# A fused attention and expert-layer kernel: four operand tiles moved by 32 bytes against the 64-byte lines of the weights

## The chip, the cores and the metric

The program runs on one NeuronCore of a Trainium2 chip. Its metric is the device time of one execution in microseconds. One execution was taken by the hardware profiler; its rows are quoted below. PE is TensorE (matmuls), PEld its weight loads, DVE is VectorE, ACT is ScalarE, POOL is GpSimd, SP is the engine that issues most DMAs.

## The reference

Input x is 2 x 2048 x 1024 in float32.

1. A convolution over the sequence with 3 taps, 1024 channels in and 768 out; its output is cut into q, k and v of 256 channels each.
2. Block attention: blocks of 128 tokens, 16 heads of 64. `qh = q @ wq + bq`, the same for k and v; scores scaled by 1/8, causal mask, softmax, `o = p @ v`; the heads' outputs times `wo` plus `bo` (256 wide), then `@ proj_w + proj_b` (1024 wide).
3. `x = layernorm(x + attention)`.
4. `base = x @ W_base.T + b_base`; a gate softmax over 8 experts minus a threshold, clipped and normed; `h = x @ A` (8 experts of rank 16), weighted by the gate, times `B`, times 2.
5. `out = layernorm(x + base + moe)`.

## The kernel before

**Products in two parts.** Every float32 operand of a large product is split into HI (`activation(Copy)` to float32r by ACT) and LO (raw minus HI, by DVE or POOL), and the product is made in three passes, `PASSES = ((HI, HI), (HI, LO), (LO, HI))`. A `matmul(out, stationary, moving)` is two instructions in the trace: a weight load (PEld) of the stationary operand, 128 x 128, and a MATMUL that streams the moving operand, 256, 266, 384 or 512 columns. Both read SBUF. The load for the next matmul runs while the matmul before it streams.

**Stages.** (a) Convolution, about 14 to 455 us: three sweeps over 4 units of 1024 tokens, 4 steps of 2 channel chunks each (48 steps of 72 matmuls, line 598), with 256 columns, stationary from `weights`, moving from `x_split`. (b) Attention, about 455 to 1035 us: `tile(t)` for 8 tiles of 512 tokens, each with 8 head pairs `s`. Per pair PE does: project_qk of the pair after next (line 1119: 6 matmuls into bankh for k and 6 into banka for q; stationary the weights, moving the split convolution tile `cs`), make_scores (line 1133), weigh_v (line 1158), transpose_probs (line 1145), project_v (line 1104: stationary `cs`, moving the weights), add_out (line 1168: stationary `wo`, moving the heads' outputs `oT`). (c) The last stage, about 1035 to 1620 us: 32 blocks of 128 tokens. Per block PE does: base (line 1525: stationary the transposed block `x1T`, moving the weights `wf`, in column ranges of 512, 384 and 266, each over 8 chunks and 3 passes), transpose_x1 (line 1515), transpose_h (line 1534), project (line 714: stationary `ys`, the tile `y_split`, moving `wp`), experts (line 1542: stationary `hT`, the tile `h_weighted_T`, moving `wb`).

**Order.** Each engine runs a program of its own, written out by hand; semaphores join them. No planner decides anything.

**Where things lie.** All large weights lie in one tile, `weights` (`attn.arena`), first the convolution's, later those of attention, `cs`, and those of the last stage, each at an offset written in the code. The tile begins at byte 16512 of a partition (a multiple of 64, and of 128). Behind it come the staging tiles and small ones, and then `scratch`, at byte 145728 (a multiple of 64, and 64 past a multiple of 128), in which `attn.at(name, ..., offset)` places everything else by hand. So before the change, modulo 64 bytes: the convolution weights 0, `x_split` 0, the attention weights 0, `cs` 0, `oT` 0, `x1T` 0, `hT` 0, `wb` 0, `wp` 0, `y_split` 32, `identity` 32, the first x1 tile (`v_bias_rows`) 32, the second (`x_odd`) 0. A row of `wf` is 1162 elements (4648 bytes), so its chunks begin at 0, 16, 32, 48, 0, 16 (HI, chunks 0 to 5) and 40, 56, 8, 24, 40, 56 (LO); chunks 6 and 7 lie in `late_weights` at 0 and 16 (HI), 40 and 56 (LO).

Of the kernel before, what the change touches and what calls it, by code (L numbers as in the profile page):

```python
# [8 lines left out]
F32 = mybir.dt.float32  # L9
F32R = mybir.dt.float32r  # L10
# [4 lines left out]
P = 128  # L15
BATCH, SEQ, DM = 2, 2048, 1024
# [8 lines left out]
ST = 512  # L25
# [4 lines left out]
CC = DM // P  # L30
CF = 3 * WB // P
KC = WB // P
HP = HEADS // 2
XS = 3
WCOLS = DM + ER + EXPERTS + 2
# [9 lines left out]
FP = CF // 2  # L45
CHUNK = 2 * 2 * CF * P
ARENA = CC * CHUNK
MASK_ROWS = P // QUAD
MASK_STORES = QUAD
SCRATCH = 20880  # L50
SMALL = 79968
SCORE_SMALL = 80128
Phase = namedtuple("Phase", "sync gpsimd scalar vector tensor")
# [13 lines left out]
class AttentionStart:  # L67
# [7 lines left out]
    NW = KC * HE  # L75

    def __init__(self, ctx, nc):
        def sb(name, shape, dt):
            return ctx.enter_context(nc.sbuf_tensor(name, shape, dt))

        def sem(name):
            return ctx.enter_context(nc.semaphore(name))

        NW, TILE = self.NW, CF * ST
        self.banks = [ctx.enter_context(nc.psum_tensor(f"bank{chr(97 + i)}", [P, ST], F32)) for i in range(8)]
        self.arena = sb("weights", [P, ARENA], F32R)
        self.stages = sb("weight_stage", [P, 2 * WCOLS], F32)
        self.stage = self.stages[:, 0:NW]
        self.craw = sb("conv_tile", [P, CF, ST], F32)
        self.out = sb("features_out", [P, KC, ST], F32)  # L90
        self.mask = sb("causal_mask", [P, P], F32)
        self.ident = sb("identity", [P, P], F32)
        self.bq, self.bk = sb("q_bias", [P, HP], F32), sb("k_bias", [P, HP], F32)
        self.bv, self.bo = sb("v_bias_rows", [P, HE], F32), sb("o_bias", [P, KC], F32)

        self.start = [2 * NW * n for n in range(3)] + [6 * NW + 2 * TILE]
        self.w = [self.arena[:, a:a + 2 * NW].rearrange("p (i n) -> p i n", i=2) for a in self.start]
        self.cs = self.arena[:, 6 * NW:6 * NW + 2 * TILE].rearrange("p (i f n) -> p i f n", i=2, f=CF)

        self.bias_loaded = sem("attn_bias_loaded")  # L100
        self.wv_loaded, self.stage_loaded = sem("wv_loaded"), sem("weight_stage_loaded")
        self.w_hi, self.w_lo = sem("attn_w_hi"), sem("attn_w_lo")
        self.zeroed, self.masks = sem("attn_zeroed"), sem("attn_masks")
        self.c_loaded = sem("conv_tile_loaded")
        self.c_hi, self.c_lo = sem("conv_tile_hi"), sem("conv_tile_lo")
        self.stored = sem("stored")
        self.y_stored = [sem(f"conv_y_stored{i}") for i in range(2)]
        self.evac, self.fin_done = sem("conv_evacuated"), sem("conv_finished")

        self.base = (nc.sbuf_base + 31) // 32 * 32  # L110
        sb("scratch", [P, SCRATCH], F32)
        self.nc = nc

    def at(self, name, shape, dt, offset):

        assert 0 <= offset and offset + 4 * math.prod(shape[1:]) <= 4 * SCRATCH, name
        return self.nc.alloc_sbuf_tensor_at(name, shape, dt, offset=self.base + offset)


def conv_phase(ctx, nc, xT, conv_w, conv_b, convT, attn, attn_w, q_bias, k_bias, v_bias, o_bias):  # L120
# [30 lines left out]
    def sem(name):  # L151
        return ctx.enter_context(nc.semaphore(name))

    w = attn.arena[:].rearrange("p (c i k n) -> p c i k n", c=CC, i=2, k=2)
    craw = attn.craw[:].rearrange("p f n -> p (f n)")
    wraw = [craw[:, 0:TAPS * KTAPS].rearrange("p (k n) -> p k n", k=TAPS),
            attn.stages[:, 0:TAPS * KTAPS].rearrange("p (k n) -> p k n", k=TAPS)]
# [7 lines left out]
    mbuf = attn.at("conv_m", [P, 2, 2 * 2 * UQ], F32, 36864)  # L165
    mask4 = attn.at("mask_by_phase", [MASK_ROWS, QUAD, P], F32, 77888)
    bias = attn.at("conv_bias", [P, CF], F32, 79936)
# [41 lines left out]
    def sync(sp):  # L209
# [75 lines left out]
        def store_masks():  # L285
            sp.wait_ge(attn.masks, MASK_STORES + 1)
            for r in range(MASK_STORES):
                sp.dma_start(attn.mask[r * MASK_ROWS:(r + 1) * MASK_ROWS, :], mask4[:, r, :]).then_inc(stored, 16)

# [58 lines left out]
    def gpsimd(pool):  # L348
# [4 lines left out]
        for r in range(QUAD):  # L353
            rows = mask4[:, r, :].rearrange("p (k n) -> p k n", k=QUAD)
            nc.gpsimd.affine_select(out=rows, in_=rows, compare_op=ALU.is_ge, fill=MASKED, base=r,
                                    pattern=[[-1, QUAD], [-QUAD, MASK_ROWS]],
                                    channel_multiplier=QUAD).then_inc(attn.masks, 1)
# [80 lines left out]
    def vector(dve):  # L438
# [85 lines left out]
        def finish_second(u, p):  # L524
# [7 lines left out]
            else:  # L532
                dve.wait_ge(y_stored[e % 2], 32 * (e // 2))
            a = m[(FP * u + p) % 2].rearrange("p f k (b j) -> p f k b j", j=MASK_ROWS)
            l = L[e % 2].rearrange("p i f k (b j) -> p i f k b j", j=MASK_ROWS)
            y = Y[e % 2].rearrange("p f (b k j) -> p f b k j", k=QUAD, j=MASK_ROWS)
            y = [y[:, :, :, k, :] for k in range(QUAD)]
# [100 lines left out]
class FfnStart:  # L638
# [8 lines left out]
    def __init__(self, ctx, nc, attn, proj_w, ffn_w, lora_b):  # L647
        def sem(name):
            return ctx.enter_context(nc.semaphore(name))

        def parts(a, n):
            return attn.arena[:, a:a + 2 * n].rearrange("p (i n) -> p i n", i=2)


        qk = attn.at("q_and_k", [P, 2, 2, ST], F32, 0)
        self.k, self.q = qk[:, 0, :, :], qk[:, 1, :, :]
        late = attn.at("late_weights", [P, self.LATE * 2 * WCOLS], F32R, 45056)
        second, kept = attn.start[1], CC - self.LATE
        self.wp = [parts(attn.start[attn.WV] + 2 * DM * k, DM) for k in range(KC)]
        self.wf = [parts(second + 2 * WCOLS * k, WCOLS) for k in range(kept)]  # L660
        self.wf += [late[:, 2 * WCOLS * k:2 * WCOLS * (k + 1)].rearrange("p (i n) -> p i n", i=2) for k in range(self.LATE)]
        self.wb = parts(attn.start[attn.WO] + 2 * attn.NW, DM)

        wo = attn.start[attn.WO]
        self.x1T = attn.arena[:, wo:wo + 4 * DM].rearrange("p (i h k n) -> p i h k n", i=2, h=2, k=CC)
        self.stage = [attn.stages[:, i * WCOLS:(i + 1) * WCOLS] for i in range(2)]
        self.stage.append(attn.at("weight_stage2", [P, WCOLS], F32, 63648)[:])

        f = [(ffn_w[k], self.wf[k], WCOLS) for k in range(CC)]
        p = [(proj_w[k], self.wp[k], DM) for k in range(KC)]  # L670
        self.weights = [(lora_b, self.wb, DM)] + p + f
        self.AFTER_V, self.AFTER_QK = 1, 1 + KC
        self.KEPT = len(self.weights) - self.LATE

        raw = attn.craw[:].rearrange("p f n -> p (f n)")
        self.xt = raw[:, 0:2 * DM].rearrange("p (i n) -> p i n", i=2)
        self.yr = raw[:, 2 * DM:2 * DM + 2 * KC * P].rearrange("p (i k n) -> p i k n", i=2, k=KC)
        self.ys = attn.at("y_split", [P, 2, 2, KC, P], F32R, 68320)
        self.pb = attn.at("proj_b_rows", [P, DM], F32, 72416)

        self.w_loaded = [sem(f"ffn_w_loaded{i}") for i in range(STAGES)]
        self.w_hi = sem("ffn_w_hi")
        self.w_lo = [sem(f"ffn_w_lo{n}") for n in range(len(self.weights))]
        self.pb_loaded = sem("proj_b_loaded")
        self.x_loaded = [sem(f"x_tile_loaded{i}") for i in range(2)]
        self.y_loaded = [sem(f"y_loaded{i}") for i in range(2)]
        self.xb_ready = sem("x_plus_bias_ready")
        self.y_hi, self.y_lo = sem("y_hi"), sem("y_lo")
        self.attn_stored = attn.stored
        self.proj_done = sem("proj_done")  # L690
        self.res1_ready = sem("res1_ready")


        small = attn.at("ln_small", [P, 34], F32, SMALL)
        self.stats = small[:, 0:24].rearrange("p (k h n) -> p k h n", k=2, h=2)
        self.mv = small[:, 24:28].rearrange("p (k n) -> p k n", k=2)
        self.var_eps, self.rstd = small[:, 28:30], small[:, 30:32]
        self.minus_half, self.eps = small[:, 32:33], small[:, 33:34]
        self.consts = sem("ln_consts_ready")
        self.ln_step = [sem(f"ln{k + 1}_step") for k in range(2)]  # L700
        self.var_ready = [sem(f"ln{k + 1}_var_ready") for k in range(2)]
        self.rstd_ready = [sem(f"ln{k + 1}_rstd_ready") for k in range(2)]
        self.stats_seen = sem("ln_stats_seen")
        self.x1_ready = sem("x1_ready")
        self.first_x1 = attn.bv
# [45 lines left out]
def attention_phase(ctx, nc, convT, attn, yT, ffn, x, y_blocks, proj_b):  # L751
# [11 lines left out]
    w, cs, craw = attn.w, attn.cs, attn.craw  # L763
# [4 lines left out]
    q, k = ffn.q, ffn.k  # L768
# [2 lines left out]
    ntop = attn.at("score_neg_max", [P, 2, 2 * BLK], F32, SCORE_SMALL + 64)  # L771
    total = attn.at("prob_sum", [P, 2, 2 * BLK], F32, SCORE_SMALL + 128)
    inv = attn.at("prob_inv_sum", [P, 2, 2 * BLK], F32, SCORE_SMALL + 192)
    oT = attn.at("heads_out", [P, 2, 2, ST], F32R, 36864)
    probsT = attn.at("probs_T", [P, 2, ST], F32, 32768)
    y = attn.out[:, 0:KC, :]
    ps_qt, ps_kt = attn.banks[0], attn.banks[7]
# [452 lines left out]
def ffn_phase(nc, x, yT, attn, ffn, b_base, b_thr, out):  # L1230

    with ExitStack() as ctx:
# [20 lines left out]
        wts = attn.at("gate_weights", [P, EXPERTS], F32, 33536)  # L1253
        wsum = attn.at("gate_sum", [P, 3], F32, 33568)
        hw = attn.at("h_weighted", [P, ER], F32, 33600)
        hT = attn.at("h_weighted_T", [P, 2, P], F32R, 34112)
        ps_a = attn.banks[0:2]
        ps_f = [attn.banks[2:5], attn.banks[5:8]]
        HT0 = LAST
# [409 lines left out]
```

## Time and profile before

| | |
|---|---|
| median of 3 runs | 1622.99 us (1621.26 to 1624.43) |
| the profiled execution | 1622.18 us, its span 1620.1 us |
| PE busy | 1555.3 us, 96% of the span, 10816 matmuls |
| PEld busy | 1387.3 us, 86% |
| DVE busy | 1183.7 us, 73% |
| ACT busy | 610.4 us, 38% |
| POOL busy | 263.4 us, 16% |

The span runs from the first to the last instruction; the device time is 2.1 us longer. A matmul's recorded duration holds a part that overlaps the next matmul, so what one costs in a dense stretch is the spacing from start to start, which the views of the timeline give.

### The profile page before, as it was taken

What the parts mean: (1) busy time and instruction counts of PE and PEld (TensorE: products, weight loads), DVE (VectorE), ACT (ScalarE), POOL (GpSimd) and SP (SyncE); (2) the same over time, 40 slices, a digit from 0 to 9 for tenths busy, and PEclk for the clock granted to TensorE, in tenths of its full rate; (3) what the DMA queues carried; (4) which work ended last, traced back from release to release, by engine and by line L of the source; (5) the groups of instructions that cost most, each with busy time, mean ns of one, the idle gap of its engine ahead of it and who ended that gap; (6) DMA issues with size and microseconds to landing.
All of it is one profiled execution on the core that took longest, in us unless ns stands there. A gap on an engine that the chain in (4) does not pass through costs nothing. (4 is left out here: it accounts for less than half of the span.)

```text
span 1620.1 us, 29293 instructions
## 1 busy us (share of the span) xinstructions
PE 1555.3 (96%) x10816; PEld 1387.3 (86%) x10816; DVE 1183.7 (73%) x2785; ACT 610.4 (38%) x1729; POOL 263.4 (16%) x230
## 2 busy tenths in 40 slices
PE   6998999699979999999999999899999999999997
PEld 6998999699968878888888888789898989998997
DVE  6858867687686666666666667777888788878884
ACT  4223322322257676676777677511111111111110
POOL 0000000000011010100101011533333333333331
PEclk9999999799999999999999999899999999999999
DMA  7887664677850001010110112412111211121111
GB/s 293 327 291 267 215 220 167 213 259 266 287 197 7 24 31 52 0 52 0 52 52 0 52 58 83 134 59 75 59 58 63 82 59 58 58 84 62 58 43 52
DMA packets 55157, 181.05 MB, mean 112 GB/s; under 512 B 5552, under 2 KB 13872, under 8 KB 48432
## 3 DMA queue, kind: packets, MB, share of 16 engines
q1 hardware_dynamic: 53360, 173.81, 30.6%
q10 hardware_dynamic: 1728, 6.29, 1.0%
q8 instruction: 47, 0.77, 0.2%
q14 instruction: 22, 0.18, 0.0%
HBM read 125.49 MB, written 54.53 MB: 111 GB/s over the span
## 5 line engine op out<-in xcount | busy, mean ns | idle before, releaser
L919 ACT ACTIVATE scores_and_probs<-scores_and_probs,score_neg_max 128x128 f32<-128x128 f32 x512 | 198.1, 393 | 1.6 <-DVE score_neg_max L1017 1.6
L1012 DVE CUSTOM_DVE_ANT_0 scores_and_probs<-bankb,causal_mask 128x128 f32<-128x128 f32 x256 | 59.2, 287 | 119.1 <-PE bankc L1133 116.7
L1361 ACT ACTIVATE gate_exp<-h_and_gate,gate_neg_max 128x8 f32<-128x8 f32 x32 | 9.6, 301 | 348.9 <-DVE gate_neg_max L1436 348.9
L366 ACT ACTIVATE x_split<-x_planes 128x1024 fp32r<-128x1024 f32 x48 | 51.0, 1062 | 202.4 <-PE bankf L598 152.7
L1104 PE MATMUL bankg<-weights 128*128 128x512 f32 x384 | 106.1, 412 | 1.8 <-DVE v_heads L1002 1.5
L886 POOL TENSOR_TENSOR weights<-conv_tile,weights 128x1024 fp32r<-128x1024 f32 x14 | 35.8, 2556 | 435.4 <-ACT weights L905 350.4
L486 DVE TENSOR_TENSOR x_split<-x_planes,x_split 128x1024 fp32r<-128x1024 f32 x48 | 58.7, 1222 | 64.2 <-ACT x_split L366 63.9
L1119 PE MATMUL bankh<-weights 128*128 128x512 f32 x384 | 99.0, 393 | 1.4 <-DVE weights L561 1.4
L1119 PE MATMUL banka<-weights 128*128 128x512 f32 x384 | 98.3, 391 | 0.7
L598 PE MATMUL banka<-x_split,weights 128*128 128x256 f32 x576 | 79.0, 285 | 20.3 <-DVE weights L508 14.2
L919 ACT ACTIVATION_READ_ACCUMULATOR scores_and_probs<-scores_and_probs,score_neg_max 128x1 f32 x512 | 98.3, 192 | 0.0
L598 PE MATMUL banke<-x_split,weights 128*128 128x256 f32 x576 | 77.6, 282 | 21.1 <-ACT conv_m L399 12.8
L598 PEld LDWEIGHTS banka<-x_split,weights 128*128 128x128 f32 x576 | 72.7, 193 | 22.2 <-issue 22.1
L598 PEld LDWEIGHTS banke<-x_split,weights 128*128 128x128 f32 x576 | 72.2, 192 | 21.6 <-ACT conv_m L399 13.0
L1119 PEld LDWEIGHTS bankh<-weights 128*128 128x128 f32 x384 | 72.0, 188 | 18.9 <-DVE weights L561 1.8
L1119 PEld LDWEIGHTS banka<-weights 128*128 128x128 f32 x384 | 71.5, 188 | 18.6 <-POOL weights L886 3.3
L731 DVE BATCH_NORM_STATS2 ln_small<-residual_sum 128x6 f32<-128x512 f32 x126 | 81.1, 685 | 5.9 <-DVE residual_sum L725 4.6
L879 POOL TENSOR_TENSOR weights<-weight_stage,weights 128x512 fp32r<-128x512 f32 x4 | 6.9, 1750 | 464.7 <-ACT weights L983 464.7
L1024 DVE TENSOR_TENSOR scores_and_probs<-scores_and_probs,prob_inv_sum 128x1024 f32<-128x1024 f32 x64 | 80.4, 1256 | 2.2
L1133 PEld LDWEIGHTS bankb<-q_and_k 64*128 64x128 f32 x512 | 61.7, 187 | 22.6 <-issue 22.6
L1104 PEld LDWEIGHTS bankg<-weights 128*128 128x128 f32 x384 | 68.3, 191 | 14.2 <-DVE v_heads L1002 2.0
L598 PE MATMUL bankb<-x_split,weights 128*128 128x256 f32 x576 | 77.5, 282 | 0.0
(229 smaller groups left out, 3975.0 us busy)
## 6 DMA issues: line engine op xcount, KB each, us to landing
x_raw<-in_xT SPq DMA_DIRECT2D x32, 1028.0 KB, 7.2
conv_tile<-in_x SPq DMA_DIRECT2D x32, 512.0 KB, 3.7
out<-out_tile SPq DMA_DIRECT2D x32, 512.0 KB, 2.7
conv_tile<-convT_scratch SPq DMA_DIRECT2D x16, 768.0 KB, 6.5
conv_tile<-in_conv_w SPq DMA_DIRECT2D x8, 1152.0 KB, 7.4
weight_stage<-in_conv_w SPq DMA_DIRECT2D x8, 1152.0 KB, 9.3
ce_scratch<-conv_l SPq DMA_DIRECT2D x16, 512.0 KB, 8.4
x_planes<-ce_scratch SPq DMA_DIRECT2D x16, 512.0 KB, 4.5
```

What stands on the lines that cost most here:

```text
L366: nc.scalar.activation(xs[:, j % XS, HI], T[:, j % 2, 0:2], ACT.Copy).then_inc(x_hi, 1)
L486: nc.vector.tensor_tensor(xs[:, j % XS, LO], T[:, j % 2, 0:2], xs[:, j % XS, HI].bitcast(F32), ALU.subtract).then_inc(x_lo, 1)
L598: last = nc.tensor.matmul(acc[f][:, k, :], w[:, c, a, k, f * P:(f + 1) * P], xs[:, j % XS, b, k, c % CPG, :], start=(c == 0 and k == 0 and ...
L731: nc.vector.bn_stats(self.stats[:, k, h, :], src[:, h * ST:(h + 1) * ST]).then_inc(step, 1)
L886: nc.gpsimd.tensor_tensor(cs[:, LO, a:b, :], craw[:, a:b, :], cs[:, HI, a:b, :].bitcast(F32), ALU.subtract).then_inc(c_lo, 1)
L919: last = nc.scalar.activation(probs[:, s % 2, i, :], probs[:, s % 2, i, :], ACT.Exp, bias=ntop[:, s % 2, i:i + 1], scale=SCORE_SCALE, accu ...
L1012: last = nc.vector.tensor_tensor_reduce(out=probs[:, s % 2, i, :], in0=ps_s[h][:, n * P:(n + 1) * P], in1=mask[:], scale=1.0, scalar=LOWES ...
L1024: nc.vector.tensor_tensor(probs[:, s % 2, :, :], probs[:, s % 2, :, :], inv[:, s % 2, :].unsqueeze(2).broadcast_to([P, 2 * BLK, P]), ALU.m ...
L1104: last = nc.tensor.matmul(ps_v[:], cs[:, a, V[0] + kc, b * P:(b + 1) * P], wqkv(attn.WV, c, kc, cols), start=(i == 0), stop=(i == 5))
L1119: last = nc.tensor.matmul(out[:], wqkv(weight, a, kc, slice(s * P, (s + 1) * P)), cs[:, c, part[0] + kc, :], start=(i == 0), stop=(i == 5))
L1133: last = nc.tensor.matmul(ps_s[j][:, cols], q[rows(j), s % 2, cols], k[rows(j), s % 2, cols], start=True, stop=True)
L1361: nc.scalar.activation(ge[:], hg[:, ER:ER + EXPERTS], ACT.Exp, bias=ngm[:, 0:1], accum_out=den[:, 0:1]).then_inc(ge_ready, 1)
```

## The change

The tile `weights` grows by 32 elements (128 bytes), and with it everything behind it moves by 128 bytes. `scratch` gets 30 elements shorter. `ODD` is 8 elements (32 bytes), `LINE` 16 elements (64 bytes).

- `cs` begins `ODD` later: modulo 64 bytes it is at 32, the attention weights at 0.
- `oT` (`heads_out`) goes from offset 36864 to 36896: at 32.
- `x1T` begins `LINE + ODD` later: at 32. `hT` goes from 34112 to 34144: at 32.
- `wo`, `wb` and the convolution weights move by one or two `LINE`s; `late_weights`, `weight_stage2`, `y_split` and `proj_b_rows` move by 64 bytes inside `scratch`. Modulo 64 these stay where they were; modulo 128 the convolution weights go from 0 to 64 while `x_split` stays at 64.

No instruction is added, taken away or put in another order, and no loop, wait, size or queue differs.

```diff
+ODD, LINE = 8, 16
-SCRATCH = 20880
+SCRATCH = 20850
-        self.arena = sb("weights", [P, ARENA], F32R)
+        self.arena = sb("weights", [P, ARENA + 2 * LINE], F32R)
-        self.start = [2 * NW * n for n in range(3)] + [6 * NW + 2 * TILE]
+        self.start = [2 * NW * n for n in range(3)] + [6 * NW + 2 * TILE + LINE]
-        self.cs = self.arena[:, 6 * NW:6 * NW + 2 * TILE].rearrange("p (i f n) -> p i f n", i=2, f=CF)
+        self.cs = self.arena[:, 6 * NW + ODD:6 * NW + ODD + 2 * TILE].rearrange("p (i f n) -> p i f n", i=2, f=CF)
-    w = attn.arena[:].rearrange("p (c i k n) -> p c i k n", c=CC, i=2, k=2)
+    w = attn.arena[:, LINE:LINE + ARENA].rearrange("p (c i k n) -> p c i k n", c=CC, i=2, k=2)
-        late = attn.at("late_weights", [P, self.LATE * 2 * WCOLS], F32R, 45056)
+        late = attn.at("late_weights", [P, self.LATE * 2 * WCOLS], F32R, 45120)
-        self.wb = parts(attn.start[attn.WO] + 2 * attn.NW, DM)
+        self.wb = parts(attn.start[attn.WO] + 2 * attn.NW + LINE, DM)
-        self.x1T = attn.arena[:, wo:wo + 4 * DM].rearrange("p (i h k n) -> p i h k n", i=2, h=2, k=CC)
+        self.x1T = attn.arena[:, wo + ODD:wo + ODD + 4 * DM].rearrange("p (i h k n) -> p i h k n", i=2, h=2, k=CC)
-        self.stage.append(attn.at("weight_stage2", [P, WCOLS], F32, 63648)[:])
+        self.stage.append(attn.at("weight_stage2", [P, WCOLS], F32, 63712)[:])
-        self.ys = attn.at("y_split", [P, 2, 2, KC, P], F32R, 68320)
-        self.pb = attn.at("proj_b_rows", [P, DM], F32, 72416)
+        self.ys = attn.at("y_split", [P, 2, 2, KC, P], F32R, 68384)
+        self.pb = attn.at("proj_b_rows", [P, DM], F32, 72480)
-    oT = attn.at("heads_out", [P, 2, 2, ST], F32R, 36864)
+    oT = attn.at("heads_out", [P, 2, 2, ST], F32R, 36896)
-        hT = attn.at("h_weighted_T", [P, 2, P], F32R, 34112)
+        hT = attn.at("h_weighted_T", [P, 2, P], F32R, 34144)
```

## Rows read from the trace of the kernel before

**Rows 1.** The page, parts 1 and 2: PE's busy time and its 40 slices.
```profile
PE 1555.3 (96%) x10816; PEld 1387.3 (86%) x10816; DVE 1183.7 (73%) x2785; ACT 610.4 (38%) x1729; POOL 263.4 (16%) x230
...
PE   6998999699979999999999999899999999999997
...
PEclk9999999799999999999999999899999999999999
```
**Rows 2.** Busy time by stretch: length, engines, granted clock, DMA share, GB/s.
```profile
26.00:94.00 68.00, 66.83 (x569) 66.38 (x568) 53.12 (x72) 21.58 (x25) 0.00 (x0) 1.00 0.89 341
...
500.00:980.00 480.00, 479.25 (x3522) 388.57 (x3521) 315.66 (x1273) 335.49 (x1137) 40.65 (x16) 1.00 0.09 32
1060.00:1580.00 520.00, 520.00 (x2937) 468.52 (x2936) 420.69 (x779) 66.34 (x202) 180.06 (x173) 1.00 0.18 63
```
**Rows 3.** The page, part 4: the chain that ended last, by engine.
```profile
PE 36%; DVE 0%; POOLq 0%; issue 0%; POOL 0%; DVEq 0%
```
**Rows 4.** Timeline of PE in attention: start us, length us, line, tiles, count.
```profile
882.13 0.86 PE L1168 MATMUL banke<-heads_out,weights 128*128 128x512 f32 x3
882.83 0.86 PE L1168 MATMUL bankf<-heads_out,weights 128*128 128x512 f32 x3
883.53 1.54 PE L1119 MATMUL bankh<-weights 128*128 128x512 f32 x6
884.91 1.52 PE L1119 MATMUL banka<-weights 128*128 128x512 f32 x6
```
**Rows 5.** Matmuls of 512 columns by line: count, duration in ns min/median/max, first and last start.
```profile
L1119 PE MATMUL bankh<-weights x384: 387/393/534, 456.6 to 1005.1; 128*128 128x512 f32 x192
L1119 PE MATMUL banka<-weights x384: 387/389/504, 458.1 to 1006.5; 128*128 128x512 f32 x192
...
L1168 PE MATMUL bankf<-heads_out,weights x192: 390/394/398, 498.8 to 1030.3; 128*128 128x512 f32 x192
...
L1104 PE MATMUL bankg<-weights x384: 387/395/775, 453.6 to 995.1; 128*128 128x512 f32 x192
...
L714 PE MATMUL bankb<-weights,y_split x180: 392/394/399, 1055.5 to 1580.4; 128*128 128x512 f32 x180
```
**Rows 6.** The same view of the last stage, lines 1525 and 1542.
```profile
L1525 PE MATMUL bankc<-weights x288: 388/394/403, 1043.4 to 1589.2; 128*128 128x512 f32 x144
L1525 PE MATMUL bankd<-weights x288: 332/337/423, 1049.8 to 1594.7; 128*128 128x384 f32 x144
L1525 PE MATMUL banke<-weights x288: 280/285/340, 1040.5 to 1584.3; 128*128 128x266 f32 x144
...
L1525 PE MATMUL bankc<-late_weights,weights x96: 387/392/402, 1047.6 to 1590.5; 128*128 128x512 f32 x96
L1525 PE MATMUL bankd<-late_weights,weights x96: 331/334/338, 1053.1 to 1595.8; 128*128 128x384 f32 x96
L1525 PE MATMUL banke<-late_weights,weights x96: 280/290/292, 1042.7 to 1585.1; 128*128 128x266 f32 x96
...
L1542 PE MATMUL bankc<-weights,h_weighted_T x48: 389/395/398, 1056.9 to 1596.4; 128*128 128x512 f32 x48
```
**Rows 7.** Groups in 1206.1 to 1210.8 us: chunks 0, 2 and 6 of `wf`; busy, mean ns.
```profile
L1525 PE MATMUL bankf<-weights 128*128 128x512 f32 x3 | 0.9, 397 | 0.0
...
L1525 PE MATMUL bankf<-weights 128*128 128x512 f32 x3 | 0.9, 394 | 0.0
...
L1525 PE MATMUL bankf<-late_weights,weights 128*128 128x512 f32 x3 | 0.8, 391 | 0.0
```
**Rows 8.** Line 598 in two stretches of the convolution: min/median/max ns.
```profile
L598 PE MATMUL bankb<-x_split,weights x36: 276/281/281, 69.9 to 88.6; 128*128 128x256 f32 x36
...
L598 PE MATMUL bankb<-x_split,weights x36: 276/276/281, 103.7 to 121.9; 128*128 128x256 f32 x36
```
**Rows 9.** Transposes of the last stage against `identity`: min/median/max ns.
```profile
L1515 PE MATMUL banka<-identity,v_bias_rows x60: 272/272/273, 1067.0 to 1573.0; 128*128 128x128 f32 x60
...
L1515 PE MATMUL banka<-identity,x_odd x56: 272/273/273, 1085.1 to 1555.0; 128*128 128x128 f32 x56
```

## The prediction

> **What bounds the kernel now.** I read the page first: PE is busy 96% of the span and its slices are at 9 nearly throughout, at the full granted clock [rows 1]. The table of stretches says where it counts: in attention PE is busy 479.25 of 480 us, in the last stage 520.00 of 520, against 315.66 and 420.69 for DVE and 335.49 and 66.34 for ACT [rows 2]; the chain that ended last is PE for its whole 36% of the span, which is the last stage [rows 3]. The convolution is nearly as dense, 66.83 of 68 us, with DMA at a share of 0.89 beside it [rows 2]. So a nanosecond per matmul is a nanosecond per matmul of the end, in attention and behind it; the convolution passes it on only while DMA keeps up.
>
> The change touches no instruction, only addresses. The question is therefore what a matmul costs and whether that depends on where its operands lie. The timeline gives the spacing: line 1168 does 3 matmuls in 0.70 us (882.13 to 882.83), 233 ns each; line 1119's k part does 6 in 1.38 us, 230 ns [rows 4]. Their recorded durations are 394 and 393 ns [rows 5], so a duration is the spacing plus about 162 ns, and differences of durations are differences of cost. I use durations from here.
>
> Matmuls of one shape do not cost the same: with 512 columns they go from 387 to 399 ns, with medians of 389 (q projection), 393 (k), 394 (line 1168, and line 714 with y_split) and 395 (lines 1104 and 1542) [rows 5, 6]. In the convolution the same instruction runs at 276 in one stretch and at 281 in another, with the same operands relative to a line [rows 8]. So something lets a matmul run at two levels or between, and neither the shape nor the address alone picks it. Each matmul streams while the next one's weights are loaded; that these two reads get into each other's way is the plain reading, and it is what moving one of them could change.
>
> **What the rows say of 32 bytes.** There are places where the offset of 32 stands already. Line 714 has y_split at 32 against wp at 0: median 394, lowest 392, no better than line 1168 at offset 0 and worse than the q projection, also at 0 [rows 5]. In line 1525 chunk 2 of wf begins at 32 (HI) and 8 (LO): mean 394; chunk 0 at 0 and 40: 397; but chunk 6, at 0 and 40 as well: 391 [rows 7]. The same phase stands 3 ns above and 3 ns below the offset of 32. The transposes take 272 and 273 ns with identity and source both at 32, and with one at 32 and one at 0 [rows 9]. So the trace shows no law "32 apart is cheap"; it shows levels into which a sequence of matmuls settles.
>
> The Trainium skill speaks against the change altogether: its page "SBUF — State Buffer", section "Who interferes with whom", gives PE two independent SBUF read ports, one for the moving operand and one for weight loads, and says PE never waits on anyone. By that rule no address matters, and the sum would be 0. The rows agree for the transposes [rows 9] and not for the two levels of line 598 [rows 8], which need some cause.
>
> **The change part by part.** The trace has no row of the new placement, so each term is bounded by the lowest and highest durations of its own shape; I take the middle between the two levels that rows show as medians, 389 and 394, that is 391.5, because moving an operand draws the level anew and nothing favours one.
>
> - k and q projection (moving cs at 32): 384 x (393 - 391.5) = 0.6 us gained and 384 x (391.5 - 389) = 1.0 lost: +0.4. Bounds: all at 387, -3.1; all at 398, +5.4.
> - v projection (stationary cs): the first matmul of each six starts after another wait, so 320 count: 320 x (391.5 - 395) = -1.1. Bounds -2.6 and +1.0.
> - add_out, line 1168 (moving oT): 384 x (391.5 - 394) = -1.0. Bounds -2.7 and +1.5.
> - Line 1525, 512 columns (stationary x1T): 576 from weights x (391.5 - 394) = -1.4; 192 from late_weights x (391.5 - 392) = -0.1. Bounds -5.0 and +3.5.
> - 266 columns: ends 280 and 292, middle 286: 576 x (286 - 285) = +0.6, 192 x (286 - 290) = -0.8. Bounds -4.8 and +4.4.
> - 384 columns: medians 337 (338 in bankg) and 334, lowest 331, highest 346 in line 1542 with this shape; no second level is visible, so I take 0. Bounds -4.3 and +7.2.
> - Line 1542 (stationary hT): 96 x (391.5 - 395) = -0.3; bounds with its 384-column part -1.4 and +1.1.
> - Convolution: weights and x_split keep their phase in 64 bytes, though their distance in 128 bytes changes from 64 to 0. I take 0. If placement decides its level after all, each of its 12 units of 288 matmuls can flip by 5 ns, 1.4 us; the medians are 281, so at least half is at the upper level: from -17 to +8.6. Kept as a tail.
> - The writers of the moved tiles (ACT for HI, DVE and POOL for LO): no row shows the new placement. In attention DVE is idle 164 us of 480 and ACT 145, in the last stage DVE 99 of 520 [rows 2], which hides a third more time on ACT and DVE in attention and a fifth on DVE behind it; without that cover each per cent on DVE's 315.66 us would be 3 us. Taken as 0. No DMA touches cs, oT, x1T or hT; weight_stage2 and proj_b_rows are loaded once.
>
> Sum: 0.4 - 1.1 - 1.0 - 1.5 - 0.2 - 0.3 = -3.7 us. From the profiled execution's own 1622.2 us that is 1618.5; the median shown is 0.8 above that execution, so 1619.3, and I say **1619**. Bounds without the convolution: about -24 and +24, 1599 and 1647.
>
> **The rivals.** A: *the offset really keeps the reads apart*, and every changed product falls to the lowest duration of its shape. That is the -24 in full; 387 and 280 are reached today by single matmuls, so a real effect would bring most of them there, say 14 us: 1609 (between 1599 and 1615). For it: spacing varies by up to 12 ns within one line with nothing else changed. Against it: y_split and chunk 2 [rows 5, 7]. B, on the other side: *the q and k projections lose the level they have settled in*. They are the cheapest today, and moving cs puts them and their neighbours at the top of their shape: 384 x 9 + 384 x 5 = 5.4 us for line 1119, 1.5 for line 1168, 1.0 for line 1104, 7.9 together: 1631. It decides as soon as the q projection's median rises from 389 to about 396. For it: line 714, with an offset of 32, never goes under 392. Against it: it must hit three lines at once. C: *the change doesn't do what it says*, since addresses play no part (the page's rule above): 1623, and every median stays.
>
> **How the numbers follow.** Forecast 0.38, A 0.30, B 0.20, C 0.12. The forecast's own range is 1614 to 1625. The range of 8 in 10 goes from 1604 to 1631: it leaves out the lower end of A, a strong B, and a convolution that flips as a whole. Under 0.2% (3.2 us) a difference is none that a measurement of this kernel tells from no change. Faster by more: all of A and half of the forecast, 0.30 + 0.20 = 0.50. Within: 0.15 of the forecast and C, 0.27. Slower: B and the rest, 0.23.
>
> **What would show it right or wrong.** Counts stay at 10816 matmuls. By the forecast line 1119's banka rises from 389 towards 391 or 394, line 1168 falls below 394, and line 1525 has medians within 3 ns of today's. By A the medians of 1119, 1168, 1104 and 1525 go to 387 to 389 together, and line 714, whose offset is unchanged, stays at 394. By B 1119 goes to 396 or more. By C nothing moves by over 1 ns. I am wrong altogether if line 598 changes level in most units, or if PE is no longer busy 479 of 480 us in attention.

## The result: 13 us slower, and the time is in the convolution

| | median of the runs | against before |
|---|---|---|
| before | 1622.51 us (1619.04 to 1624.43, 6 runs) | |
| after | 1635.68 us (1633.74 to 1639.65, 6 runs) | ratio 1.0084, 95% interval 1.0068 to 1.0100 |

The profiled execution of the kernel after took 1639.65 us, the longest of its six and 4.0 us above their median; its span is 1637.7 us. The instruction counts are the same. The page of the kernel after answers to [rows 1] with this; the last two lines are PE's slices and its granted clock:

```profile
PE 1570.5 (96%) x10816; PEld 1398.7 (85%) x10816; DVE 1183.9 (72%) x2785; ACT 610.5 (37%) x1729; POOL 262.6 (16%) x230
...
PE   6999899699989999999999999899999999999998
...
PEclk9999999899999999999999999999999999999999
```

PE is busy 15 us longer for the same 10816 matmuls, and its granted clock reads nearly alike in both. Where, the view by line tells (count, min/median/max duration in ns, first and last start). First the convolution after, to [rows 8]:

```profile
L599 PE MATMUL banka<-x_split,weights x576: 278/283/550, 14.0 to 461.7; 128*128 128x256 f32 x192
L599 PE MATMUL bankb<-x_split,weights x576: 277/283/415, 15.4 to 463.1; 128*128 128x256 f32 x192
```

The median went from 281 to 283, which looks small. But the lowest went from 276 to 277 or 278, and the fast stretches are gone. The last start of banka in the convolution was 446.0 us before and is 461.7 now: 15.7 of the 17.6 us of span are lost before attention begins. The timeline of one step of the kernel after gives the spacing (start, length, line, tiles, count):

```profile
99.83 1.48 PE L599 MATMUL bankb<-x_split,weights 128*128 128x256 f32 x11
101.15 1.60 PE L599 MATMUL bankc<-x_split,weights 128*128 128x256 f32 x12
102.59 0.88 PE L599 MATMUL bankd<-x_split,weights 128*128 128x256 f32 x6
```

Bankc's 12 matmuls take 102.59 - 101.15 = 1.44 us, 120.0 ns each. The kernel before shows two spacings, 1.41 us and 1.36 us for 12 matmuls, 117.5 and 113.3 ns each:

```profile
76.96 1.58 PE L598 MATMUL banka<-x_split,weights 128*128 128x256 f32 x12
78.37 0.87 PE L598 MATMUL bankb<-x_split,weights 128*128 128x256 f32 x6
...
94.15 1.52 PE L598 MATMUL banka<-x_split,weights 128*128 128x256 f32 x12
95.51 0.84 PE L598 MATMUL bankb<-x_split,weights 128*128 128x256 f32 x6
```

Taken from the starts of all matmuls of the trace, with the gaps over 130 ns left out (waits), every one of the 48 steps is at 120.0 ns (119.6 at the least); before, 26 steps were at 117.8, 21 near 113.3 and one between. Mean 119.9 against 115.8. Here and below, the first step of a unit can lie some ns off its level.

Then attention and the last stage after, to [rows 5, 6]:

```profile
L1120 PE MATMUL bankh<-weights x384: 389/396/497, 472.3 to 1023.6; 128*128 128x512 f32 x192
L1120 PE MATMUL banka<-weights x384: 388/396/500, 473.8 to 1025.0; 128*128 128x512 f32 x192
...
L1169 PE MATMUL bankf<-heads_out,weights x192: 388/397/420, 514.5 to 1048.8; 128*128 128x512 f32 x192
...
L1105 PE MATMUL bankg<-weights x384: 389/394/774, 469.5 to 1013.4; 128*128 128x512 f32 x192
...
L715 PE MATMUL bankb<-weights,y_split x180: 394/396/400, 1072.7 to 1597.9; 128*128 128x512 f32 x180
...
L1526 PE MATMUL bankc<-weights x288: 387/394/407, 1060.6 to 1606.6; 128*128 128x512 f32 x144
L1526 PE MATMUL bankd<-weights x288: 331/337/426, 1066.9 to 1612.2; 128*128 128x384 f32 x144
L1526 PE MATMUL banke<-weights x288: 282/286/338, 1057.6 to 1601.8; 128*128 128x266 f32 x144
...
L1526 PE MATMUL bankc<-late_weights,weights x96: 392/396/398, 1064.8 to 1608.0; 128*128 128x512 f32 x96
```

The q projection's median rose from 389 to 396, k's from 393 to 396. Line 1526 has the medians of before within 1 ns where it reads `weights`; against `late_weights` with 512 columns it rose from 392 to 396, and with 266 it fell from 290 to 286. Summed over starts: q +2.3 us, k +0.9, line 1526 +0.8 with 512 columns (all of it against `late_weights`) and -0.5 with 384 and 266, the other lines together -1.4. PE is as full as before in both stages:

```profile
500.00:980.00 480.00, 479.29 (x3512) 386.37 (x3510) 313.69 (x1272) 332.67 (x1126) 40.47 (x16) 1.00 0.10 34
1080.00:1600.00 520.00, 520.00 (x2932) 467.65 (x2932) 420.07 (x782) 66.36 (x202) 177.14 (x171) 1.00 0.19 63
```

So nearly all of the loss is in a stage that the change was not aimed at. In the tables below the **distance** is the start of the moving operand minus the start of the stationary one, exactly, in bytes modulo 256. For x_split and the convolution weights it was 158016 - 16512 = 141504, which is 192; after the change it is 158144 - 16576 = 141568, which is 0. (All steps inside the two tiles are multiples of 512.)

### The profile page after: what moved, and what is told of

The parts are those of the page before. It is cut to its first block and busy times, and to the rows that moved or that the text cites. A ratio compares the mean times of both kernels' runs of the same rounds, so it can differ in the third digit from the quotient of the medians.

```text
span 1637.7 us, 29293 instructions
## 1 busy us (share of the span) xinstructions
PE 1570.5 (96%) x10816; PEld 1398.7 (85%) x10816; DVE 1183.9 (72%) x2785; ACT 610.5 (37%) x1729; POOL 262.6 (16%) x230
## 5 line engine op out<-in xcount | busy, mean ns | idle before, releaser
L1013 DVE CUSTOM_DVE_ANT_0 scores_and_probs<-bankb,causal_mask 128x128 f32<-128x128 f32 x256 | 59.2, 287 | 121.8 <-PE bankc L1134 119.3
L1120 PEld LDWEIGHTS bankh<-weights 128*128 128x128 f32 x384 | 71.7, 188 | 19.6 <-DVE weights L562 1.6
L599 PE MATMUL bankb<-x_split,weights 128*128 128x256 f32 x576 | 80.8, 288 | 0.0
```

What stands on the lines that cost most here:

```text
L599: last = nc.tensor.matmul(acc[f][:, k, :], w[:, c, a, k, f * P:(f + 1) * P], xs[:, j % XS, b, k, c % CPG, :], start=(c == 0 and k == 0 and ...
L1013: last = nc.vector.tensor_tensor_reduce(out=probs[:, s % 2, i, :], in0=ps_s[h][:, n * P:(n + 1) * P], in1=mask[:], scale=1.0, scalar=LOWES ...
L1120: last = nc.tensor.matmul(out[:], wqkv(weight, a, kc, slice(s * P, (s + 1) * P)), cs[:, c, part[0] + kc, :], start=(i == 0), stop=(i == 5))
```

## The experiments

The theory, D: a matmul's spacing follows from the distance between what it streams and the weights loaded beside it, in more than a 64-byte line. The rivals: the 32-byte moves cost the time (E), any shift of scratch does (F), or the levels are chance of timing (T).

**1. The convolution's distance undone in the kernel after**, but not exactly: it becomes 64, where the kernel before has 192.

```diff
-    xs = attn.at("x_split", [P, XS, 2, 2, CPG, UQ], F32R, 12288)
+    xs = attn.at("x_split", [P, XS, 2, 2, CPG, UQ], F32R, 12352)
```

with the convolution's other tiles behind it, and the small ones, 128 bytes later.

> The kernel after, with one thing undone: x_split starts 64 bytes later in the scratch tile (the tiles of the convolution behind it 128 bytes later, to make room), so that it is again 64 bytes away from the convolution weights modulo 128. Theory D (the distance of the moving operand from the next weights, taken modulo 128 bytes, sets the spacing of a matmul): the convolution's spacing goes from 120.0 back to a mix of 113.3 and 117.8 ns, its 3456 matmuls take about 439 us in place of 455, the whole 1620 to 1624 us. Rival E (the 32-byte moves of cs, heads_out, x1T and hT are what costs, and the convolution merely varies from program to program): the convolution stays where it is or varies by itself, the whole stays at 1636 us. Rival F (any shift of scratch by 128 bytes costs): stays at 120.0 ns and 1636 us.

Measured 1629.03 us (9 runs), ratio 1.0035 (1.0014 to 1.0056): about half of the way back, and 5 us above the 1620 to 1624 expected. The 120.0 is gone from all steps: 35 steps at 117.8, 12 at 113.3 and one between in the profiled execution. Its runs spread from 1620.85 to 1633.03. E and F fail on the convolution; D holds with a mix that is not that of before.

**2. The same distance as after, made in the kernel before.** x_split at 12352 there, nothing of attention or of the last stage touched.

> The kernel before, with x_split alone put 64 bytes further (the convolution's tiles behind it 128 bytes further), so that its distance from the convolution weights is 0 modulo 128 as in the kernel after; cs, heads_out, x1T, hT untouched. Theory D: all 48 steps of the convolution at 120.0 ns, +16 us, 1638 to 1640 us, and the q projection stays at 227 ns. Rival E: 1622 us and a mix of 113.3 and 117.8. Rival F: 1622 us.

All 48 steps at 120.0 ns; the last steps of the timeline read as in the kernel after:

```profile
99.79 1.60 PE L598 MATMUL bankd<-x_split,weights 128*128 128x256 f32 x12
101.23 1.60 PE L598 MATMUL banke<-x_split,weights 128*128 128x256 f32 x12
102.67 0.76 PE L598 MATMUL bankf<-x_split,weights 128*128 128x256 f32 x5
```

The time is 1630.74 us (6 runs), ratio 1.0041 (1.0023 to 1.0059), less than the 1638 to 1640 expected: 3456 x 4.1 ns is 14 us of spacing, its convolution's sum of starts rose by 10.9 (439.5 to 450.4) and the execution by 9.7. The waits in the convolution got shorter by the rest, from 39.2 to 35.9 us. In the medians it is +7.4 us (1623.31 beside it). The profiled execution of the kernel after has the same 120.0 ns and still a sum of 455.5, since its waits are 41.0 us; it is that kernel's slowest run, and what lengthened them is not shown. The convolution's other tiles moved too, by 128 bytes; experiment 9 moves them by the same and x_split by 16 bytes less, and the 120.0 is gone. So it is the move of x_split that makes the slow convolution.

**3 and 4. Two more distances, and cs.** The kernel after with x_split at 32, cs back at 0; and with x_split at 96, cs at 64.

```diff
-        self.cs = self.arena[:, 6 * NW + ODD:6 * NW + ODD + 2 * TILE]
+        self.cs = self.arena[:, 6 * NW + 0:6 * NW + 0 + 2 * TILE]
```

(16 in place of 0 in the second.)

> The kernel after with two moves in two stages, each read in its own: x_split 32 bytes later (32 from the convolution weights modulo 128), and cs at 0 from the attention weights again. Theory D: the q projection is back at 227 ns from 233.6 (line of 384 matmuls, about -2.3 us) and k at 230 from 232.7; the convolution takes a level of its own, which an account by 64-byte lines (odd is good) puts at 113.3 or less and an account by 128 only anywhere from 113.3 to 120. Rival E': the q projection's level comes from what runs around it (oT, wo moved by 64 bytes), then it stays at 233 ns.

> The kernel after with x_split 96 bytes later (96 from the convolution weights modulo 128) and cs at 64 from the attention weights. Theory D: if only the distance modulo 64 counts, this convolution equals that at 32, and the q projection equals cs at 0, 227 ns; if modulo 128 counts, they may differ, and the q projection goes to a level like line 1168's before, 233 ns, whose moving operand was 64 from its weights. Rival: all levels are chance of timing, then convolution steps show a mix of levels whatever the distance.

1633.67 and 1633.25 us (one run each). The convolution is at 116.7 and 117.8 in whole units at distance 32. At 96 single matmuls take 116 to 125 ns in turn, and every step has a mean of 119.8 to 120.1, the level of distance 0:

```profile
100.61 1.60 PE L599 MATMUL bankd<-x_split,weights 128*128 128x256 f32 x12
102.05 1.36 PE L599 MATMUL banke<-x_split,weights 128*128 128x256 f32 x10
```

32 and 96 are not equal, so 64 bytes are not the period. q is at 228.9 ns with cs at 0 and 229.5 with cs at 64, against 233.6 at 32: the move of cs by 32 is what slowed it. But 228.9 is not the 227.2 of before; perhaps what runs ahead of it (line 1169, with oT and wo moved) has a say, which no run shows.

**5 to 8. Other distances in all lines at once.** Each line is read by itself. In these four the rows of wf are also padded, so that all chunks begin at one phase modulo 128. (Not modulo 256: a padded row is 4736 bytes, 18.5 times 256, so HI and LO rows lie 128 apart.)

```diff
+WPITCH = (WCOLS + 31) // 32 * 32
-        self.wf = [parts(second + 2 * WCOLS * k, WCOLS) for k in range(kept)]
+        self.wf = [parts(second + 2 * WPITCH * k, WPITCH)[:, :, 0:WCOLS] for k in range(kept)]
```

> The layout of the kernel after, with other distances (moving minus stationary, modulo 128 bytes), each stage read by itself: convolution 80, k and q projection 16, v projection 112, add_out 16, and in line 1526's place the weight rows padded to 4736 bytes so that all chunks of wf have one phase, distance 0. Theory D (the distance sets the level or the few levels of a line): each line shows one or two spacings; base with 512 columns settles at 227 ns in place of 225 to 236, as the q projection does at distance 0, its sum falls by about 768 x 4.5 = 3.5 us. Rival T (levels are chance of timing, the distance plays no part): base stays at a mean of 231.7 ns and the convolution mixes 113.3 and 117.8.

> As the one before, with distances: convolution 48, k and q projection 48, v projection 80, add_out 48, base 64 with padded rows, experts 64. Theory D: base with 512 columns goes to 233 ns, as add_out at 64 in the kernel before; the convolution lies between 113.3 and 120 with one level per unit. Rival T: as above, no difference between this and the one before.

> As before, with distances: convolution 112, k and q projection 56, v projection 72, add_out 0, base 32 with padded rows, experts 96. Theory D: add_out at 0 goes from 233 to 227 ns, 384 x 6 = -2.3 us; base with 512 columns at the q projection's level for 32, 233 ns. Rival T: add_out stays at 233.

> As before, with distances: convolution 16, k and q projection 8, v projection 120, add_out 64, base 16 with padded rows, experts 80. Theory D: add_out back at 233.4 as in the kernel before; the convolution at 16 near its 120 at distance 0, or between that and 117 at 32. Rival T: a mix of 113.3 and 117.8 in the convolution.

| | time | convolution: distance, mean ns, steps | q at, mean | add_out at, mean | base 512 at (modulo 128), mean |
|---|---|---|---|---|---|
| u_a | 1631.35 | 80: 119.3, 118.3 or 120.0 by unit | 16: 231.3 | 16: 231.2 | 0: 230.0 |
| u_b | 1634.50 | 48: 118.3, all steps | 48: 231.7 | 48: 231.6 | 64: 231.4 |
| u_c | 1616.37 | 112: 113.4, all steps | 56: 232.8 | 0: 230.7 | 32: 231.5 |
| u_d | 1620.21 | 16: 116.6, 113.3 or 118.7 by unit, one unit 116.7 | 8: 233.5 | 64: 231.6 | 16: 232.0 |

(One run each; before took 1618.60 beside them. u_b's convolution has a mean 1.0 ns under u_a's and still a sum of starts 0.7 us above it; the rest is waits.) Rival T falls: the convolution shows its own levels at each distance. Part of what D was to give is refuted as well: add_out at 0 came to 230.7, not to the 227 that the q projection has there, so the distance alone does not fix the level of a short run between other work. For base the test was none. Its mean is 230.0 to 232.0, as with unpadded rows (231.2), but no kernel had it at one distance modulo 256. In u_a its HI times HI matmuls take 231.1 ns from `weights` and 235.0 from `late_weights`, placed alike modulo 128 and 128 apart modulo 256. What the distance rules plainly is the long uniform run of the convolution. And u_c shows a distance at which all 48 steps take 113.3.

**9 to 12. That distance in the kernel before, and the rest of the change alone.** Four kernels, of which three were run 12 times each: the kernel before with x_split 48 bytes further, the kernel after with x_split 112 further, the same with cs back at 0, and, run once, the kernel before with x_split 176 further.

```diff
-    xs = attn.at("x_split", [P, XS, 2, 2, CPG, UQ], F32R, 12288)
+    XN = XS * 2 * 2 * CPG * UQ
+    xs = attn.at("x_split", [P, XN + 32], F32R, 12288)[:, 12:12 + XN].rearrange(
+        "p (s i k c n) -> p s i k c n", s=XS, i=2, k=2, c=CPG)
```

(12 elements here; 28 in the kernel after, 44 in the last.)

> The kernel before with x_split alone 48 bytes later, 112 from the convolution weights modulo 128; everything of attention and the last stage as before. Theory D: all 48 steps of the convolution at 113.3 ns, whatever runs around them, in place of the mix of 113.3 and 117.8: 3456 x (115.8 - 113.4) = 8.3 us of spacing, of which some goes into waits, so 1614 to 1617 us against 1622.5, and a smaller spread from run to run, since the mix is what varies. Rival G (113.3 in the kernel that had 112 came from its other moves): the mix comes back, 1620 to 1624 us.

> The kernel after with x_split at 112 from its weights. The convolution is then the same as in the kernel before with 112, and the difference of the two is what the moves of cs, heads_out, x1T, hT and wo are worth by themselves. Theory D: +2.3 (q) +0.7 (k) +0.8 (line 1526 with 512 columns) -0.8 (266 and 384 columns) and about -1 (other lines): +1.5 to +3 us, 1616 to 1619. Rival E (the 32-byte moves were most of the slowdown): +6 us or more against the kernel before with 112.

> As the one before, with cs back at 0 from the attention weights. Theory D: q from 233.6 to about 229, k from 232.7 to 231, together 1.9 + 0.6 us, so 2 to 3 us faster than the one before and within 1 us of the kernel before with 112. Rival: the two projections are hidden behind other engines, then no difference.

> The kernel before with x_split 128 bytes further than in the one with 112, so 240 from the weights modulo 256 and still 112 modulo 128. Theory D with a period of 128 bytes: all 48 steps at 113.3 ns again. Rival: the period is longer, then another level or mix.

I had counted modulo 128, where the kernel before stands at 64. Exactly it stands at 192, so 48 more is 240 and 176 more is 112, and the texts of the first and the fourth have the two exchanged. The results bear on the period:

| | distance | steps | median, ratio and interval |
|---|---|---|---|
| before, x_split +48 | 240 | 117.1, all | 1624.89; 1.0020 (1.0008 to 1.0032) |
| after, x_split +112 | 112 | 113.3, all | 1618.72; 0.9978 (0.9966 to 0.9989) |
| the same, cs at 0 | 112 | 113.3, all | 1617.16; 0.9967 (0.9958 to 0.9977) |
| before, x_split +176 | 112 | 113.3, all | 1616.04, one run |

112 and 240 are the same modulo 128 and differ, 113.3 against 117.1 ns: 128 is refuted as a period. At 240 the timeline has 1.41 us for 12 matmuls, where at 112 it has 1.36 (shown at the end of this section):

```profile
100.58 1.57 PE L600 MATMUL banke<-x_split,weights 128*128 128x256 f32 x12
101.99 1.45 PE L600 MATMUL bankf<-x_split,weights 128*128 128x256 f32 x11
```

The expectation for the first of the four (1614 to 1617) was missed by 8 us for that reason. The q projection, by the view of groups (busy us, mean ns of one), first of the kernel after with x_split +112:

```profile
L1122 PE MATMUL banka<-weights 128*128 128x512 f32 x384 | 100.6, 397 | 0.7
```

and with cs at 0 as well:

```profile
L1122 PE MATMUL banka<-weights 128*128 128x512 f32 x384 | 98.9, 392 | 0.7
```

The move of cs is shown in the spacing (233.6 to 228.9 for q, 232.7 to 231.3 for k, 2.3 us together). The medians differ by 1.6 us in the direction of that. Their intervals against before overlap, but of the 12 runs with cs at 0 ten lie under 1617.9, and of the 12 with cs at 32 eleven lie above it, so the whole time shows the move too.

**13 to 15. What was still open.**

> The same kernel as the one that was looked at once with x_split 176 bytes further, timed in rounds. Counted exactly, x_split minus the convolution weights is 368 bytes modulo 512 here and in the three kernels after with x_split at 112; in the kernel before with x_split 48 bytes further it was 240, which is 112 modulo 128 as well and gave 117.1 ns. Theory D' (the distance counts modulo more than 128 bytes, 256 or 512): 113.3 ns in all 48 steps again, and since the rest is as before, 1.6 to 4 us faster than the kernel after with 112, 1614 to 1617 us. Rival: the rest of the change was worth nothing, 1618 to 1619 us.

> The kernel before with x_split 320 bytes further: 0 from the convolution weights modulo 512, where the kernel after has 256. If the period is 256 bytes, all 48 steps are at 120.0 ns again; if it is 512 or more, another level shows, perhaps the q projection's good one (17/16 ns per column rate, 113.3).

> The kernel after with the convolution's distance put back exactly to that of the kernel before, 192 modulo 512 (the first attempt at this had 320). Theory D': the mix of 113.3 and 117.8 ns as in the kernel before; the rest costs the +1.5 to 3 us of the moves of cs, heads_out, x1T and hT, so 1623 to 1627 us. Rival (the convolution's slowdown had another source beside the distance): 1629 us or more, as with 320.

*The period.* x_split at 0 modulo 512 (the kernel after has 256 modulo 512): all steps at 120.0 again, 1632.29 us in one run. (The 17/16 in that expectation is no price of a column: 113.3 ns for 256 columns is 0.44 ns each.)

```profile
99.79 1.60 PE L600 MATMUL bankd<-x_split,weights 128*128 128x256 f32 x12
101.23 1.60 PE L600 MATMUL banke<-x_split,weights 128*128 128x256 f32 x12
102.67 0.76 PE L600 MATMUL bankf<-x_split,weights 128*128 128x256 f32 x5
```

0 and 256 agree, 112 and 240 don't: for this line the distance counts modulo 256 as far as these four tell; that a distance and the same plus 256 agree rests on this one pair.

*Distance or address.* One more rival is that x_split's own address sets the level. It lies at 128 modulo 256 in experiments 2, 14 and 15, with 120.0 ns in the first two and the mix in the third, where the weights lie 64 bytes further. And the weights lie at 128 modulo 256 in the kernel before and in experiments 2, 9, 12, 13 and 14, with the mix, 120.0, 117.1 and 113.3 ns among them. Neither address does it alone; the distance fits all.

*The old distance exactly.* The kernel after with x_split 448 bytes further has 192 again. The old mix is back, unit for unit but for the first: its steps 0 to 2 are at 113.3 to 113.5 where 117.8 stood, and units 1, 3, 4, 6, 9 and 11 are at 117.8 (the first step of unit 4 at 116.1) as before. The median of 10 runs is 1625.03, ratio 1.0020 (1.0008 to 1.0031). That is 3.3 us above the runs of before beside it (1621.77). So of the 13.2 us some 10 come back with this one address, and 3.3 stay with everything else that the change moved. The largest part of that rest is q and k with cs at 32, together 3.2 us by their starts in the kernel after:

```profile
L1122 PE MATMUL banka<-weights 128*128 128x512 f32 x384 | 100.6, 397 | 0.7
L1122 PE MATMUL bankh<-weights 128*128 128x512 f32 x384 | 100.4, 397 | 1.3 <-DVE weights L564 1.3
```

*The version that beats both.* The kernel before with x_split alone moved by 176 bytes: 1616.09 us (6 runs, 1614.29 to 1619.56), ratio 0.9965 (0.9951 to 0.9978), 5.7 us under the runs of before beside it (1621.77) and 19.6 under the median of after. Its line 600, and its timeline at the same place, 1.36 us for 12 matmuls, 113.3 ns each:

```profile
L600 PE MATMUL bankb<-x_split,weights x576: 275/275/415, 15.6 to 441.9; 128*128 128x256 f32 x192
```

```profile
100.15 1.52 PE L600 MATMUL bankf<-x_split,weights 128*128 128x256 f32 x12
101.51 1.52 PE L600 MATMUL banka<-x_split,weights 128*128 128x256 f32 x12
102.87 0.50 PE L600 MATMUL bankb<-x_split,weights 128*128 128x256 f32 x3
```

The 8.3 us of spacing gave 5.7 in the median; the sum of the convolution's starts fell by 5.8 (439.5 to 433.7).

## Why the prediction was wrong

The forecast was 1619, its range 1604 to 1631; it came to 1635.7, outside, and slower where half of the chance lay on faster. The sign that it named for being wrong altogether, a new level in most units of line 598, came in all 12.

- **What bounds the kernel** was right: PE, at a granted clock of 1.00 in attention and behind it. There more nanoseconds per matmul came through for the most part (2.3 us of spacing with cs moved gave 1.6 in the medians), and in the convolution, which has 35 to 46 us of waits in every kernel, for half or more (14 gave 7.4, 8.3 gave 5.7).
- **Two levels, set by neither shape nor phase in 64 bytes alone** was right as far as it went. It was read as levels drawn anew by chance. In the convolution they are set by the distance modulo 256, and in a mix only where a distance allows two or three. The other lines are no lottery either: the spacing of the q projection is 227.1 to 227.3 in all six traces with the old layout of attention, and the sums of line 1525 per shape agree within 0.2 us in those six, and again in the seven with the new layout of the last stage. The trace of before held the sign: over all 32 blocks line 1525 takes 234.6 ns in chunk 0 and 228.6 in chunk 6 (96 matmuls of 512 columns each), which have one phase in 64 bytes. Their HI rows are 0 and 192 from x1T modulo 256.
- **The step that failed** is the line on the convolution: "weights and x_split keep their phase in 64 bytes, though their distance in 128 bytes changes from 64 to 0. I take 0." The change itself was seen, and put off as a tail with a bound of +8.6 us, since the highest level that the trace showed was 281. The runs put a third level there, 283 (120.0 ns), which no stretch of the kernel before shows. That term is 14 us of spacing, above the bound, and +7.4 us in the medians when made in the kernel before, about 10 when undone in the kernel after (the intervals of the two overlap). The bound was taken from rows at one distance, while the change went to another: such rows bound nothing.
- **k and q, +0.4** (bounds -3.1 and +5.4): measured +0.9 and +2.3. The "middle of two levels" was the wrong value for the cheapest line: q sat at its lowest, and could mostly lose.
- **The other lines of the sum**: add_out -1.0, measured about 0; v -1.1, measured -0.3; line 1525 with 512 columns -1.5, measured +0.8; 266 columns -0.2, measured -0.4; 384 columns 0, measured -0.1. All small, as forecast, and of mixed sign; together with k and q the medians of the kernel after with the old convolution say +3.3 where the sum said -3.7. (Its durations of 512 columns "from 387 to 399" leave out line 1525, which reaches 403 in [rows 6].)
- **Rival B** named the right place among the moved tiles and the right mark, q's median at 396, but not the time: it was to raise lines 1119, 1168 and 1104 to the top of their shape for 7.9 us; only the first rose, for 3.2 (in the second one bank's median went from 394 to 397 and the other's to 392). That its 1631 is nearer than the forecast is luck, since the loss is elsewhere.
- **Rival A** (32 bytes keep the reads apart) is refuted: the medians of 1120, 1169, 1105 and 1526 with 512 columns lie at 392 to 397, none at 387. The two rows that spoke against it, y_split and chunk 2 of wf [rows 5, 7], were read rightly.
- **Rival C** (no address matters) is refuted by experiment 2, where one address moves 48 steps. The rule of the Trainium skill behind it ("SBUF — State Buffer", section "Who interferes with whom": two independent read ports, PE never waits on anyone) does not give the cost of this line: with the same instructions its matmul takes 113.3 to 120.0 ns by the distance of the two operands. Whether it is the ports that fail to be independent, no run shows. That the two reads collide is the likeliest account, but argued only: no run here took the weight loads away. Why the distance 192 (and 64, 32, 16 and 80) allows two or more levels, which one a unit of 288 matmuls falls into, and why they hold for that long, stays open; that 11 of 12 units fell alike in the two kernels at 192 speaks against mere chance.

The Trainium skill ("TensorE: Matmul & The Clock Gate", section "Back-to-back issue gap") gives N / 2.4 + 2.5 ns as the gap of an isolated warm matmul of N columns, which makes an estimate of 109.2 for 256 columns; for a sustained stream of weight loads and matmuls it gives another figure, 131 ns for 512 columns. The traces agree with neither: the best distance found here gives 113.3 for 256 columns, and 512 columns of float32r take 227 to 235. Whether the 4 ns above 109.2 can be gained or belong to these float32r reads, no run shows.

## What to carry to other kernels

When a tile grows or moves, list the distance of every pair of operands that PE reads together, moving against the weights loaded beside it, in bytes modulo 256 (shown for the convolution's line alone), before and after; the pairs that were not meant to move count as well, and the longest uniform run of matmuls comes first. Look at starts in the timeline: a spacing that is constant within a step and jumps between steps (113.3 and 117.8) says that an address is worth trying. One profile per distance reads the level to 0.1 ns where a distance has one level, even where the whole time is too noisy. Leave out as waits only gaps that lie clear of the spread of single matmuls, which at distance 96 reached 125 ns. Bound a new placement by other placements of the same line, never by the spread at the old one.

## What the runs showed of the hardware

- Spacing of the convolution's matmuls (128 x 256, float32r, weights reloaded each time) by distance modulo 256: 0: 120.0; 16: 113.3, 116.7 or 118.7; 32: 116.7 or 117.8; 48: 118.3; 64 and 192: 113.3 or 117.8; 80: 118.3 or 120.0; 96: 120.0 in the mean of a step; 112: 113.3; 240: 117.1. Only 0, 112 and 192 were seen in more than one kernel.
- Whether the choice of level is part of the spread from run to run is not shown. With two levels nine runs span 12.2 us (64, the kernel after), and 17 and 29 runs 6.9 and 9.9 (192, the kernel before); with one level 12 runs span 5.0 to 6.9 (112 and 240). No kernel with two levels was profiled twice.
- The transposes against `identity` [rows 9] stay at 109 ns from start to start in the kernel after, and the sums of starts of the float32 products of lines 1133 and 1158 are within 0.1 us of those of before.
